# Softmax of a graph-attention kernel: 12 exponentials per tile with bias and accumulator in place of shift, one exponential and sum

## What is computed

```python
q = split_heads(x @ Wq + bq); k = ...; v = ...
scores = einsum('bhqd,bhkd->bhqk', q, k) / sqrt(HD)
scores = where(adj > 0, scores + beta * adj, -9e15)
probs = softmax(scores, axis=-1)
x = layernorm(x + einsum('bhqk,bhkd->bhqd', probs, v))
```

## Time and profile before

| What | Value |
|---|---|
| Median of three runs | 1110.32 us |
| The profiled execution | 1110.85 us, its span 1109.1 us |
| TensorE matmul busy | 1063.5 us, 96% |
| VectorE busy | 936.5 us, 84% |
| ScalarE busy | 444.9 us, 40% |
| GpSimd busy | 528.7 us, 48% |
| Share of TensorE in the chain that ended last | 90% |
| Mean granted TensorE clock | 0.985 of full speed |

### The profile page before, as it was taken

One profiled execution on the slowest core, in us unless ns is written; L12 is line 12 of the kernel. 1 busy time (PEld: TensorE's weight loads), 2 busy tenths in 40 slices (PEclk: granted clock), 3 DMA queues, 4 the chain that ended last, 5 costly groups with the idle time before them and its releaser, 6 DMA issues.

```text
span 1109.1 us, 38264 instructions
## 1 busy us (share of the span) xinstructions
PE 1063.5 (96%) x16896; PEld 917.9 (83%) x16896; DVE 936.5 (84%) x1642; ACT 444.9 (40%) x713; POOL 528.7 (48%) x454
## 2 busy tenths in 40 slices
PE   4789999999999999999999999999999999999975
PEld 3678888888888888888888888888888888888864
DVE  2468998998989899898989989898898989978785
ACT  3334443444344343444433444444444434444321
POOL 0135454454545546454454645445364544655443
PEclk8989999999999999999999999999999999999997
DMA  8103111112112011111102111111211210010101
GB/s 265 39 2 97 50 59 43 38 45 64 37 43 59 26 54 46 42 53 49 49 26 64 38 43 59 43 38 45 64 38 43 59 36 15 17 35 2 40 24 37
DMA packets 61749, 53.32 MB, mean 48 GB/s; under 512 B 35984, under 2 KB 55440, under 8 KB 61584
## 3 DMA queue, kind: packets, MB, share of 16 engines
q1 hardware_dynamic: 60752, 49.69, 15.1%
q10 hardware_dynamic: 832, 1.18, 0.3%
HBM read 38.28 MB, written 12.58 MB: 46 GB/s over the span
## 4 chain that ended last, share of the span: by engine, by line
PE 90%; DVE 4%; issue 2%; DMA 2%; ACT 1%; POOL 1%; SPq 0%; POOLq 0%; DVEq 0%; ACTq 0%
PE ps_u L340 53%; PE ps_s L357 9%; PE ps_o L340 8%; PE ps_p L425 7%; PE ps_p L440 7%; PE ps_x L370 3%; PE ps_o L454 2%; DMA xt_in<-in_x_t 1%; DVE probs L620 1%; POOL probs L756 1%; DMA bo_rows<-in_bo 1%; DVE row_sum L668 1%; DVE xt_lo L648 1%; ACT probs L547 0%; DVE row_max L630 0%
## 5 line engine op out<-in xcount | busy, mean ns | idle before, releaser
L756 POOL TENSOR_TENSOR probs<-probs,row_max 128x768 f32<-128x768 f32 x128 | 209.8, 1639 | 323.0 <-DVE row_max L630 323.0
L762 POOL TENSOR_TENSOR probs<-probs,row_inv 128x768 f32<-128x768 f32 x128 | 188.6, 1474 | 128.8 <-DVE row_inv L676 69.5
L516 ACT COPY probs_t<-ps_p 128x768 f32<-128x768 f32 x128 | 102.6, 802 | 201.3 <-PE ps_p L425 201.2
L340 PE MATMUL ps_u<-w_hi_v,xt_lo 128*128 128x384 f32 x384 | 138.4, 360 | 7.0 <-DVE v_sb L661 5.4
L668 DVE TENSOR_REDUCE row_sum<-probs 128x12 f32<-128x768 f32 x128 | 121.6, 950 | 24.4 <-ACT probs L547 23.6
L547 ACT ACTIVATE probs<-probs 128x768 f32<-128x768 f32 x128 | 108.4, 847 | 83.0 <-POOL probs L756 83.0
L340 PE MATMUL ps_u<-xt_hi,w_lo_k 128*128 128x512 f32 x288 | 119.0, 413 | 11.6 <-ACT q_sb L535 6.3
L340 PE MATMUL ps_u<-w_hi_v,xt_hi 128*128 128x384 f32 x384 | 129.9, 338 | 0.0
L340 PE MATMUL ps_u<-w_lo_v,xt_hi 128*128 128x384 f32 x384 | 129.8, 338 | 0.0
L775 POOL TENSOR_TENSOR rstd<-var_eps,minus_half 128x1 f32<-128x1 f32 x128 | 69.9, 546 | 124.9 <-DVE var_eps L709 124.9
L630 DVE TENSOR_REDUCE row_max<-probs 128x12 f32<-128x768 f32 x128 | 121.4, 948 | 2.2
(11 more groups left out here) (78 smaller groups left out, 2033.4 us busy)
## 6 DMA issues: line engine op xcount, KB each, us to landing
x_in<-in_x SPq DMA_DIRECT2D x16, 768.0 KB, 4.5
out<-z SPq DMA_DIRECT2D x64, 192.0 KB, 1.9
xt_in<-in_x_t SPq DMA_DIRECT2D x15, 768.0 KB, 4.7
adj<-in_adj SPq DMA_DIRECT2D x64, 128.0 KB, 2.9
xt_in<-in_x_t SPq DMA_DIRECT2D x3, 256.0 KB, 4.6
q_sb<-in_wq ACTq DMA_DIRECT2D x3, 192.0 KB, 4.8
k_sb<-in_wk ACTq DMA_DIRECT2D x1, 576.0 KB, 7.6
v_sb<-in_wv SPq DMA_DIRECT2D x1, 576.0 KB, 7.2
```

The source lines that it names most:

```text
L340: last = nc.tensor.matmul(dst, a(g), b(g), start=(g == 0 and n == 0), stop=(g == KT - 1 and n == 2))
L516: nc.scalar.copy(probs_t[:].rearrange("p (a i) n -> p a (i n)", a=2), ps_p[:, :, 0:KT * P]).then_inc(probs_t_ready, 1)
L756: nc.gpsimd.tensor_tensor(s, s, over_keys(row_max[p]), ALU.subtract).then_inc(shifted, 1)
L762: nc.gpsimd.tensor_tensor(s, s, over_keys(row_inv[p]), ALU.mult).then_inc(probs_ready, 1)
```

## The change

The maximum is taken negated (`minus_max`). ScalarE waits for the maximum itself and takes 12 exponentials of 64 elements, one for each head and graph; each adds its column of `minus_max` as a bias and gives the sum of its 64 results from the accumulator into its column of `row_sum`. GpSimd's subtraction and VectorE's sum of the segments are gone. The wait for the exponentials, `exp_ready`, is raised by the twelfth of them.

```diff
             def exponentials(tile):
-                act.wait_ge(shifted, at(tile) + 1)
-                e = probs[tile[2] % 2][:].rearrange("p i b k -> p (i b k)")
-                nc.scalar.activation(e, e, ACT.Exp).then_inc(exp_ready, 1)
+                p = tile[2] % 2
+                act.wait_ge(max_ready, at(tile) + 1)
+                for i in range(PAIRS):
+                    for b in range(GT):
+                        n = i * GT + b
+                        last = nc.scalar.activation(probs[p][:, i, b, :], probs[p][:, i, b, :], ACT.Exp,
+                                                    bias=minus_max[p][:, n:n + 1],
+                                                    accum_out=row_sum[p][:, n:n + 1])
+                last.then_inc(exp_ready, 1)
...
-                nc.vector.tensor_reduce(row_max[t % 2][:], rows, AX_X, ALU.max).then_inc(max_ready, 1)
+                nc.vector.tensor_reduce(minus_max[t % 2][:], rows, AX_X, ALU.max, negate=True).then_inc(max_ready, 1)
...
                 dve.wait_ge(exp_ready, at(tile) + 1)
-                nc.vector.reduce_sum(row_sum[p][:], probs[p][:].rearrange("p i b k -> p (i b) k"), AX_X)\
-                    .then_inc(sum_ready, 1)
-                dve.wait_ge(sum_ready, at(tile) + 1)
...
-            def shift(tile):
-                p = tile[2] % 2
-                pool.wait_ge(max_ready, at(tile) + 1)
-                s = probs[p][:].rearrange("p i b k -> p (i b) k")
-                nc.gpsimd.tensor_tensor(s, s, over_keys(row_max[p]), ALU.subtract).then_inc(shifted, 1)
```

More of the change, by code:

```diff
@@ L167, in two_gnn_layers_kernel @@
         minus_half = sb("minus_half", [P, 1])
-        row_max = [sb(f"row_max{p}", [P, PAIRS * GT]) for p in range(2)]
+        minus_max = [sb(f"minus_max{p}", [P, PAIRS * GT]) for p in range(2)]
         row_abs = [sb(f"row_abs{p}", [P, PAIRS * GT]) for p in range(2)]
@@ L222, in two_gnn_layers_kernel @@
         v_ready = sem("v_ready")
-        sum_ready = sem("sum_ready")
         inv_ready = sem("inv_ready")
@@ L231, in two_gnn_layers_kernel @@
         normed = sem("normed")
-        shifted = sem("shifted")
         probs_ready = sem("probs_ready")
@@ L777, in _ @@
             for s in STEPS:
-                if s.cur:
-                    shift(s.cur)
                 if s.turned:
```

## The result

The changed kernel takes 1239.66 us, the median of four runs (1238.86 to 1240.51), beside 1111.7 us for the kernel before. The ratio is 1.115, with a 95% interval of 1.1125 to 1.1175. The forecast was 1212 us in a range of 1145 to 1320. The profiled execution took 1239.14 us with a span of 1237.3, so 128.2 us were added to the span where the walk had 101.

A forecast was written before the change was run, and what follows sets the result against it. TensorE was taken as the bound between 92 and 1060 us, never waiting. New stalls of 6.34 us a cycle over 16 cycles, 101 us, on the profiled 1110.85 gave 1212.3, median 1212 us; range 1145 to 1320.

The forecast's parts named there:

- the walk: Longest path between successive copies of turned probabilities, for eight intervals (a two-chunk cycle): 6.34 us added a cycle, 101 us in all.
- the eighth interval: Last of a cycle's eight spans between copies of turned probabilities, 9.42 us before; forecast 11.05, through later k copies.
- the seventh: Span between copies of turned probabilities, 7.01 us before; the path through `scale` was to make it 7.53, +0.52.
- The price of one of the twelve: Start-to-start time of one short ScalarE exponential with bias and accumulator: 0.33 us, so twelve take 3.96 instead of 0.75.
- the read without overlap: Rival: the accumulator's read doesn't overlap on ScalarE, 0.43 us for each exponential, 1362 us in all; chance 0.12.
- Intervals 7 and 8 together: Last two spans of a cycle: later reciprocal, bias and maximum plus a longer exponential run delay k copies, +2.15 us.
- The rival that named the clock: TensorE's clock falls on top of the forecast because of new idle gaps, adding 64 us: 1276 us; chance 0.05.
- 16 cycles of one pattern: All 128 tiles counted as 16 repeats of a two-chunk pattern, 72.0 us each instead of 65.7.
- the mean per tile: Added time of 0.79 us a tile, assumed also at the program's ends, where the pattern is another.
- interval 1: Span where `o_lo` comes behind a k copy and the heads' copy: 8.74 us against 8.40, +0.34.
- interval 3: Span where `o_lo` comes behind reciprocals and a v copy: 8.70 us against 7.59, +1.11.
- the fourth interval: Span with a k copy and a q unit of 512 columns: path 9.92 us against 10.13, so 0 added.

## Why the prediction was right, and where it was short

**What bounds the kernel: right in the main.** Removing the work of GpSimd and VectorE alone gave 18 us, 1.6%. The reading that TensorE never waits between 92 and 1060 us was a little too strong. It rested on busy time, and short waits don't show there: besides the 0.26 us of the eighth interval the seventh had 0.36 us to give, 7 us over the 13 cycles.

**The price of one of the twelve: right.** 0.33 us forecast, 0.33 measured, with its parts taken apart by two experiments: 0.15, 0.09 for the bias, 0.09 for the accumulator's read. The guess was that the read is an instruction that overlaps like any other; it is one. For the read without overlap the prediction had 0.16 + 0.03, and no row stands behind the 0.03; a read measured 0.19 us in length, 0.09 of it in the stream.

**The walk: right in seven of eight intervals**, and in the wait that it named for each, `o_lo`, `v_sb`, `k_sb` or `scale`. It says 6.34 us a cycle; cycles at full clock measured 7.2 (72.88 against 65.67).

**Intervals 7 and 8 together, "+2.15": mis-sized.** At full clock they grew by 2.7, and in 8 of 13 cycles by 4.3. Two things were missing. I let `make_bias0` shift as a block, but with the subtraction gone `add_bo` on GpSimd runs straight behind `scale` and beside `make_bias0`'s second operation, which then takes 1.38 us instead of 0.75: 8 us in all. The section "SBUF: two separate sides" of the page "SBUF — State Buffer" of the Trainium skill states this lock too, for a VectorE operation with two SBUF inputs against a GpSimd one that reads SBUF. The trace agrees (1379 against 752 ns). I used it for the gain on `xt_lo` and not for the loss. That gain came, 1681 to 551 ns, and together with all other relief it was worth no more than 18 us. And the clock fell after the 2.1 us wait, 13 us in all. The rival that named the clock had given it 64 us and a chance of 0.05, with gaps under 2 us; the cause was real, its size in these cycles a fifth. The move of `add_bo` alone took the collision back in full (the eighth interval is then 10.94 us, where the walk had 11.05) and the halved clock in all but one cycle. That the clock fell because of the length of the wait is shown only as far as the table of six kernels goes.

**What the sum leaves.** 128.2 us were added and 101.4 forecast. The prediction took 16 cycles of one pattern; the pattern stands 13 times, and the other 24 tiles lie at the ends. The 13 cycles grew by 105.8 us where the walk gives 82.4. Of the 23.4 between them 13 are the clock, 7 the eighth interval at full clock, and the rest small, mainly +0.2 in interval 1 and +0.1 in interval 3. The other 24 tiles grew by 22.4 us where the mean per tile gave 19. Of this, 4.3 us lie in one interval near the end, from 6.12 to 10.42 us, in which TensorE is busy for 6.08 us and its mean clock is 0.69. The ends were not taken apart further, and that the mean per tile came so near there is in part luck: their pattern is another one.

## What to carry to other kernels

Splitting one long instruction into many for a free operand (a bias, an accumulator) costs the fixed part each time; multiply it by the count and compare with the whole, not with the instruction that is saved. On a kernel whose bound engine hardly waits, removals elsewhere are worth little (here 1.6%), and additions cost as soon as the longest path behind them exceeds the bound engine's interval. Walk the intervals one by one, since their slack differs: the same twelve exponentials cost nothing in the fourth interval and 2.1 us in the eighth at full clock. After an operation is removed from a queue, look at what now moves up in it and what it will run beside.

## What the runs showed of the hardware

A sum from ScalarE's accumulator is a second instruction, 187 to 190 ns long and 0.09 to 0.10 us in the stream. An exponential of 128x64 in a run took 0.15 us from start to start without a bias column and 0.24 us with one. A VectorE operation of 128x512 with two SBUF operands took 752 ns alone and 1379 ns (median) beside an addition on GpSimd. TensorE's clock was halved for a stretch in none of 13 cycles whose longest wait was 1.0 us, in 1 of 13 at 1.5 us, in 5 at 2.07, in 8 at 2.13, and in 12 and 13 of 13 at 2.9 us.
